# Second attention of a hybrid block: the third score term as a 64-row pass, and a mask of 192 columns

## The reference, cut to what matters

```python
# L1_attn_a, here with B, L = 4, 512 and D = 256
NQ, NKV, HD, SW = 32, 8, 64, 64;  QM = NQ // NKV
proj = x @ W_qkv                                  # x is layer-normed
q, k, v = jnp.split(proj, (NQ*HD, (NQ+NKV)*HD), axis=-1)
q = _apply_rope(q.reshape(B, L, NKV, QM, HD), ...);  k = _apply_rope(k.reshape(B, L, NKV, HD), ...)
attn = jnp.einsum('bqhmd,bkhd->bhmqk', q, k) * sm_scale
mask = (q_pos >= k_pos) & (q_pos < k_pos + SW)
attn = jnp.where(mask, -jnp.inf, attn)            # the masked band is the 64 keys up to the query itself
w = jax.nn.softmax(jnp.concatenate([attn, sink], axis=-1), axis=-1)[..., :-1]
out = jnp.einsum('bhmqk,bkhd->bqhmd', w, v).reshape(B, L, NQ*HD) @ W_out
```

## Time and profile before

| | before |
|---|---|
| time, three runs | 4045.83, 4048.83 (median), 4058.09 us |
| profiled execution, span from first to last instruction | 4055.4 us (its time around the span is not shown apart) |
| mean granted TensorE clock over the span | 0.879 |
| busy share of the span: PE, DVE, ACT, POOL | 81%, 69%, 56%, 44% |

### The profile page before, as it was taken

How to read it: one execution, slowest core, us unless ns; L and a number is a source line. 1 busy time by engine, 2 the same in 40 slices (tenths; PEclk the granted TensorE clock), 3 DMA queues, 4 the chain that set the end, 5 groups by cost and what they waited for, 6 DMA issues and landing times. The chain is left out here.

```text
span 4055.4 us, 68591 instructions
## 1 busy us (share of the span) xinstructions
PE 3283.2 (81%) x19700; PEld 2595.3 (64%) x19707; DVE 2809.6 (69%) x6227; ACT 2274.5 (56%) x5958; POOL 1766.8 (44%) x3039
## 2 busy tenths in 40 slices
PE   7799967925888489169999999999957499999575
PEld 3355556714777377058778778778745378888453
DVE  5699966646777666368858858768673378888742
ACT  3599923414777344068858868768602166666211
POOL 0299923567664045635535445446327400000165
PEclk9699977967999689579999999999956599999666
DMA  2011132440000335310000000000053500000435
GB/s 86 20 47 47 49 153 80 137 104 24 1 1 1 148 99 136 98 59 19 19 9 19 20 9 20 17 10 20 16 184 63 119 1 1 1 1 1 160 72 111
DMA packets 139453, 221.35 MB, mean 55 GB/s; under 512 B 28912, under 2 KB 114800, under 8 KB 137408
## 3 DMA queue, kind: packets, MB, share of 16 engines
q1 hardware_dynamic: 108432, 156.23, 11.6%
q0 software_dynamic: 30720, 61.44, 7.3%
HBM read 162.60 MB, written 54.80 MB: 54 GB/s over the span
## 5 line engine op out<-in xcount | busy, mean ns | idle before, releaser
L1242 POOL DMA_INDIRECT ex_xr<-scratch_rows,mo_token x288 | 287.0, 997 | 326.1 <-PE bank L1301 167.7
L596 POOL TENSOR_TENSOR sc_h<-sc_h,sc_c 128x512 f32<-128x512 f32 x256 | 327.0, 1291 | 198.1 <-DVE sc_h L633 190.1
L3034 DVE TENSOR_TENSOR sa_pT<-bank,sa_pT 128x512 fp32r<-128x512 f32 x512 | 329.9, 686 | 34.4 <-ACT sa_pT L2902 30.5
L2894 ACT ACTIVATE sa_p<-bank,sa_nm 128x512 f32<-128x512 f32 x512 | 347.0, 689 | 2.5 <-DVE sa_nm L3025 2.5
L633 DVE TENSOR_TENSOR_SCAN sc_h<-sc_da,bank 128x512 f32<-128x512 f32 x256 | 311.1, 1220 | 39.4 <-ACT sc_da L576 24.5
L2723 PE MATMUL bank<-sa_kT,sa_qT 128*128 128x512 f32 x1024 | 332.5, 436 | 1.5 <-DVE residual L3001 1.5
L3021 DVE TENSOR_REDUCE sa_mx<-bank 128x2 f32<-128x1024 f32 x256 | 312.4, 1220 | 25.7 <-PE bank L2725 22.0
L1319 PE MATMUL bank<-mo_w_gu,ex_xT 128*128 (+2 forms) x1152 | 315.7, 403 | 1.1 <-issue 0.5
L2747 PE MATMUL bank<-sa_pT,sa_v 128*128 128x256 f32 x2048 | 301.5, 290 | 16.9 <-DVE sa_pT L3034 16.5
L2747 PEld LDWEIGHTS bank<-sa_pT,sa_v 128*128 128x128 f32 x2048 | 260.2, 190 | 40.1 <-DVE sa_pT L3034 31.6
L2902 ACT ACTIVATE sa_pT<-bank 128x512 fp32r<-128x512 f32 x512 | 274.3, 585 | 7.9 <-PE bank L2735 0.7
(11 more groups left out here) (401 smaller groups left out, 9405.6 us busy)
## 6 DMA issues: line engine op xcount, KB each, us to landing
scratch_ys<-ex_yo SPq DMA_DIRECT2D x192, 128.0 KB, 2.1
mo_w_gu<-in_w_gu SPq DMA_DIRECT2D x2, 9216.0 KB, 26.8
sc_c<-scratch_c SPq DMA_DIRECT2D x64, 256.0 KB, 3.1
sa_share<-scratch_shares SPq DMA_DIRECT2D x256, 64.0 KB, 2.5
mo_w_dn<-in_w_dn SPq DMA_DIRECT2D x2, 4608.0 KB, 46.5
scratch_rows<-ln_stage SPq DMA_DIRECT2D x64, 128.0 KB, 1.9
mo_w_dn<-in_w_dn SPq DMA_DIRECT2D x2, 4096.0 KB, 34.8
ex_xr<-scratch_rows,mo_token POOLq DMA_INDIRECT x288, 2.8
```

Of the source, the lines that this page charges most:

```text
L596: pool.tensor_tensor(h, h, C[u], ALU.mult).then_inc(used.sem, 1)
L1242: pool.indirect_dma_start(xr[u][:, :], None, rows, bass.IndirectOffsetOnAxis(ap=token[:, i:i + 1], axis=0), bounds_check=rows.shape[0] - 1 ...
L2894: act.activation(pr[h][:, :], SC[2 * s_ + h][:, :], ACT.Exp, bias=nm[:, col:col + 1], scale=SCALE, accum_out=rs[:, col:col + 1]).then_inc( ...
L3034: dve.tensor_tensor(spot(1), PT[h][:, :].rearrange("p (k n) -> p k n", k=TPB), spot(0).bitcast(F32), ALU.subtract).then_inc(*inc("kept_d"))
```

## The change

Of the four products of the parts (qh kh, ql kh, qh kl, ql kl) the scores keep three. `kT[0]` now holds kh in both halves of the rows, `kT[1]` kl in both halves. `put_q` writes the even heads as (qh; ql) and the odd heads as (ql; qh). The first product of a head, 128 rows, gives qh kh + ql kh; the third term, qh kl, is a product over 64 rows alone: the upper half of the rows for the even head of a step, the lower half for the odd one. Both third products come at the end of a step's scores, after both heads' first products and masks. The mask strip is 192 columns wide instead of 256 (128, as before, in the first tile of queries). `scored` is now counted up by each third product, so a step counts two. `keep_keys` needs four ACT instructions of 64 rows instead of one of 128 and two of 64.

```diff
-    MW = 2 * P
+    MW = P + WINDOW
...
                 pool.affine_select(out=mask[:, :], in_=mask[:, :], compare_op=ALU.is_ge, fill=0.0,
-                                   base=P, pattern=[[-1, MW]], channel_multiplier=1).then_inc(*inc("made"))
+                                   base=WINDOW, pattern=[[-1, MW]], channel_multiplier=1).then_inc(*inc("made"))
...
-                                   base=WINDOW - P, pattern=[[1, MW]], channel_multiplier=-1).then_inc(*inc("made"))
+                                   base=0, pattern=[[1, MW]], channel_multiplier=-1).then_inc(*inc("made"))
...
-                        parts = qst[:, :].rearrange("p (h s d) -> p h s d", s=2, d=D)
-                        split(st, parts[:, :, 0, :], parts[:, :, 1, :], qrot[:, :], HG).then_inc(*inc("qput"))
+                        parts = qst[:, :].rearrange("p (a s d) -> p a s d", s=4, d=D)
+                        zero = c.zeros[:, :].bitcast(F32)[:, 0:D].rearrange("p (a h d) -> p a h d", a=1, h=1) \
+                            .to_broadcast([P, 2, 2, D])
+                        src = qrot[:, :].rearrange("p (a h d) -> p a h d", a=2, h=2)
+                        high, low = parts[:, :, 0:4:3, :], parts[:, :, 1:3, :]
+                        st.then(pool.tensor_tensor(high, src, zero, ALU.add))
+                        pool.tensor_tensor(low, src, high.bitcast(F32), ALU.subtract).then_inc(*inc("qput"))
...
-                        lo, hi = max(qt * P - P, 0), (qt + 1) * P
+                        lo, hi = max(qt * P - WINDOW, 0), (qt + 1) * P
                         for h in range(2):
                             bank, hh = SC[2 * s_ + h], 2 * s_ + h
-                            for w in range(2):
-                                pe.matmul(bank[:, :], qT[qt % 2][:, hh * P:(hh + 1) * P],
-                                          kT[w][:, bass.ds(g * SEQ, SEQ)], start=(w == 0), stop=False)
-                            last = pe.matmul(bank[:, lo:hi], identb[:, :], mask[:, MW - (hi - lo):MW],
-                                             start=False, stop=True)
-                        last.then_inc(*inc("scored"))
+                            pe.matmul(bank[:, :], qT[qt % 2][:, hh * P:(hh + 1) * P],
+                                      kT[0][:, bass.ds(g * SEQ, SEQ)], start=True, stop=False)
+                            pe.matmul(bank[:, lo:hi], identb[:, :], mask[:, MW - (hi - lo):MW],
+                                      start=False, stop=False)
+                        for h in range(2):
+                            bank, hh, half = SC[2 * s_ + h], 2 * s_ + h, slice(h * D, (h + 1) * D)
+                            pe.matmul(bank[:, :], qT[qt % 2][half, hh * P:(hh + 1) * P],
+                                      kT[1][half, bass.ds(g * SEQ, SEQ)], start=False, stop=True) \
+                              .then_inc(*inc("scored"))
...
-                        act.activation(spot(0), src, ACT.Copy)
+                        act.activation(spot(0)[0:D], src[0:D], ACT.Copy)
+                        act.activation(spot(0)[D:2 * D], src[0:D], ACT.Copy)
                         act.activation(spot(1)[0:D], src[D:2 * D], ACT.Copy)
-                        act.activation(spot(1)[D:2 * D], src[0:D], ACT.Copy).then_inc(*inc("kkept"))
+                        act.activation(spot(1)[D:2 * D], src[D:2 * D], ACT.Copy).then_inc(*inc("kkept"))
...
-                        dve.wait_ge(*at("scored", N + 1))
+                        dve.wait_ge(*at("scored", N * 2 + 2))
```

More of the change, by code:

```diff
@@ L3102, in sinks @@
                 kturned=TILES * 2, kkept=TILES * 2, vput=TILES, klow=TILES, qp=NQ, qraw=NQ, own_q=NQ * 3, qput=NQ,
-                qturned=NQ, qkept=NQ, scored=NP, maxed=NP, negged=NP, exped=NP * 2, turned=NP * 2, kept_a=NP * 2,
+                qturned=NQ, qkept=NQ, scored=NP * 2, maxed=NP, negged=NP, exped=NP * 2, turned=NP * 2, kept_a=NP * 2,
                 kept_d=NP * 2, summed=NP, ylow=NP, yadded=NP, sunk=NQ, sink_exped=NQ, own_n=NQ, normed=NQ,
```

## The result

| | before | after |
|---|---|---|
| median, 4 runs each | 4050.65 us | 4077.47 us (4075.13 to 4081.19) |
| ratio, 95% interval | | 1.0064 [1.0049, 1.0079] |
| span of the profiled execution | 4055.4 us | 4077.5 us |
| mean granted TensorE clock | 0.879 | 0.883 |

The change makes the kernel slower by 0.64%. The forecast was 4057 and "the same" the likeliest case; what came is the rival in which the array drains at each switch between full and half rows and the two third terms run at once, priced at 4079. The time lies inside the range, but 20 us above the forecast and outside the 4052 to 4061 that the prediction gave the forecast by itself: the range holds it only because its upper end was drawn past that rival.

A forecast was written before the change was run, and what follows sets the result against it. The prediction took the ring through `values`, `low_y`, `high_p` or `add_y` and `low_p`, not PE, as the bound. Steps 0, keys 6 and clock 2 made 8 us more, 4057 on the median of 4048.8; range 4047 to 4092.

The forecast's parts named there:

- the rival in which the array drains at each switch between full and half rows: Before `values` in even steps: x = 0.17 with both third terms at once, 22 us, time 4079; else 4137; chance 0.30.
- What sets the step: In every step, DVE's `low_p` and not PE's work lets `values` open; a pair of steps takes 7.50 us.
- the ring: Loop of `values`, `low_y`, `high_p` or `add_y`, `low_p`, next `values` across PE, ACT, DVE; sets the step, 7.50 per pair.
- No gain from cheaper scores: In the scores on PE, a saving between 0 and 0.23 us per step shortens nothing; taken as 0 us.
- x: PE's change per step: 0 to -0.23 us from the scores; above 0 even steps lengthen, from 0.17 odd ones too.
- The switch between full and half rows: On PE, in and out once a step: taken as 0 us, far bound 0.40 if the array empties each time.
- Which steps pay: For a PE loss: even steps have nothing in hand and lengthen by x, odd ones have 0.17 in hand.
- The mask, POOL: Mask at 192 columns on PE and the split into other column blocks on POOL: 0 each.
- The keys and the clock: Extra ACT key copies lengthen PE's `keep_q` wait and the first batch, 6 us; slower clock on products behind it, 2.
- The sum: Whole kernel: 0 in the steps, 6 at the keys, 2 by the clock, 8 us more, 4057.

## Why the prediction was right or wrong

- *What sets the step.* Right. `values` in odd steps still opens 0.05 behind `low_p`, and cutting the ring, without taking any work away, gave 22.5 us. In the even steps of mid-batch, ring and PE's work take the same time, 3.82 and 3.83, so that cutting either one alone gains nothing there.
- *No gain from cheaper scores.* The two thirds at once save the 0.23 that was given as the far end of x. Whether that alone would have gained nothing was not seen, since x came out above zero.
- *The switch between full and half rows.* **This step failed.** It was taken as 0 by the transpose of 4 columns in the earlier trace rows, "the only row with a change of shape"; the far bound, 0.40, was worked out from a tail of 0.16 at either end and an exposed weight load of 0.08. Measured, half rows against full rows with the thirds one after the other both times, it is 0.38: 0.15 on the way in (2426.77 to 2426.95 with half rows, 2426.78 to 2426.81 with full ones), and on the way out 0.11 between the thirds and the projection (0.66 instead of 0.55) and 0.11 more in the projection, whose first weight load comes late. A change in the number of columns is no stand-in for a change in the number of rows. So x, PE's change per step, is 0.38 - 0.23 = 0.15, the rival's 0.17 nearly. The Trainium skill, page "TensorEngine Tiling (Array Packing)", section Key Properties, says that a change of tiling mode drains TensorE; the runs agree that the switch costs time, and put the 0.38 beside it. It was quoted ahead of the result and set aside for a row that wasn't about rows.
- *Which steps pay.* Even steps have no slack and pay, odd steps pay next to nothing (3.69 for 3.67): right. The rival charged 0.17 in 128 even steps, 22 us; measured are 14.6. The size is one part: most even steps grew by 0.13 (3.82 to 3.95), those of the first tile of queries by 0.10. The number is the other: 28 even steps of a batch grew, not 32. At the end of a batch `values` has no projection in front and stays hidden behind `low_p`: from 2929.47 to 2933.29 in PEld's timeline after, the even step takes 3.82 as before.
- *The mask, POOL.* Nothing, right; the mask alone was run, and the new split on POOL is in the run with full rows, whose steps are no longer than before.
- *The keys and the clock.* 6 + 2 predicted, 7.9 measured. The wait for `keep_q` grew by 1.19 (1.22 was the term) in three batches, 3.6. From the end of that wait to the end of the products the three batches took 1.45 + 9.07, 0.81 + 7.07 and 1.21 + 8.31 before, 27.92, and take 3 x 1.45 + 24.91 = 29.26 after: 1.3 for the clock, where 2 was taken. In the first batch the scores start at 1781.97 instead of 1778.70 in PE's timelines, 3.3 for 2.4; what the layers ahead varied by is in that number.
- *The sum.* 8 was right for what it covered; the 14.6 in the steps were missing. The chance of 0.30 for the drain was too low with a far bound computed at 0.40 and no row of the right kind against it. Had the middle of 0 and 0.40 been taken, x would have been -0.03, and the step still undecided; only the far bound gave the measured time.
- *Luck.* That the rival's 4079 is within 2 us of the result is partly luck: it put 22 + 8 = 30 us on a median of 4048.8, where the traces show 14.6 + 7.9 = 22.5 and the medians 26.8.

What stays open: how much of the way out is the array emptying and how much the weight load that comes late. No run separates them. Nor was it tried on the chip whether a longer half-row stretch (the thirds of several steps together) would carry one switch for more work.

## What to carry to other kernels

Two half-row passes at once save the time of one, here 0.23 us at 512 columns, but a way into half rows and out again costs 0.38: leave the rows full, or gather several such passes behind one switch, which no run here tried. When a cost has a far bound that decides the result and no row of the same kind stands against it, the near bound should not be taken from a row that only looks alike. And before cutting an engine's work, see whether it is the work or the order that sets the step: here an order alone gave 0.6%.

## What was not expected of the hardware

- The way in and out of half-row passes costs 0.38 us at full clock between a mask and a projection, and about as much between transposes and a long pass. By the Trainium skill, page "TensorE: Matmul & The Clock Gate", Part 2, TensorE's queue pulls weight loads ahead of matmuls in flight where the rows they use don't conflict or the load goes to a background buffer. Across this switch the trace shows no such lead: behind half rows the projection's first load and the projection start together (2425.53), behind full rows the load starts 0.23 ahead (2427.13 and 2427.36).
- Idle time shown before an instruction behind half-row passes is not all spare, even where another engine's semaphore is named as its end: of 0.33, about 0.09 could be used, in two different runs. What is to be had is read on PE from start to start: 0.52 where PE waits for DVE, 0.43 where it waits for nobody.
